# Folding conditioned weights by column half as they arrive, with the folded bias formed as columns

## The reference

```python
def _L0_cond_ref(x, y, weight, mask, bias):        # y: (2, 8), weight: (8, 256, 256)
    masked_w = weight * mask[None, :, :]
    w_bot = jnp.einsum('bg,got->bot', y, masked_w)
    return jnp.einsum('bnt,bot->bno', x, w_bot) + bias

x = x + _L0_attn_ref(_L0_cond_ref(x, cond_8, ...), wq, wk, wv, wo)   # 2 heads of 128, rotary on half of each, causal
x = x + _L0_ffn_ref(_L0_cond2_ref(x, cond_8, ...), Wg, W1, W2)
x = x + _L1_attn_ref(_L1_cond_ref(x, cond_8, ...), ...)
x = x + _L1_ffn_ref(_L1_cond2_ref(x, cond_8, ...), ...)
```

## Time and profile before

| | |
|---|---|
| median of 3 runs | 930.83 us (929.63 to 931.91) |
| the profiled execution | 928.71 us, span 927.4 us |
| TensorE busy | 911.9 us, 98% of the span |
| VectorE busy | 525.9 us, 57% |
| ScalarE busy | 443.8 us, 48% |
| GpSimd busy | 270.5 us, 29% |
| TensorE busy from 29 to 60 us | 29.37 of 31 us |
| VectorE busy from 5 to 25 us | 16.75 of 20 us |

### The profile page before, as it was taken

One profiled execution on the slowest core, in us unless ns is written; L12 is line 12 of the kernel. 1 busy time (PEld: TensorE's weight loads), 2 busy tenths in 40 slices (PEclk: granted clock), 3 DMA queues, 4 the chain that ended last, 5 costly groups with the idle time before them and its releaser, 6 DMA issues.

```text
span 927.4 us, 13114 instructions
## 1 busy us (share of the span) xinstructions
PE 911.9 (98%) x4859; PEld 768.5 (83%) x4859; DVE 525.9 (57%) x974; ACT 443.8 (48%) x827; POOL 270.5 (29%) x242
## 2 busy tenths in 40 slices
PE   8999999999999999999999999999999999999998
PEld 4768868887799999998888888888888888888886
DVE  6754454578657666686665564334333335787644
ACT  3665566434255455573444343353343443335775
POOL 1533221300466675654410162041140230010000
PEclk9999999999999999999999999999999999999999
DMA  8030001220355443432503003003003012000011
GB/s 301 30 114 23 24 2 69 103 85 24 81 127 177 137 134 127 126 114 81 181 23 139 21 23 136 1 1 136 1 0 137 1 38 99 1 0 1 1 46 46
DMA packets 22193, 67.47 MB, mean 73 GB/s; under 512 B 4515, under 2 KB 11955, under 8 KB 19315
## 3 DMA queue, kind: packets, MB, share of 16 engines
q1 hardware_dynamic: 16546, 40.15, 11.9%
q0 software_dynamic: 5440, 26.50, 9.7%
q10 hardware_dynamic: 144, 0.00, 0.0%
HBM read 55.09 MB, written 9.45 MB: 70 GB/s over the span
## 4 chain that ended last, share of the span: by engine, by line
PE 91%; DVE 4%; ACT 1%; DMA 1%; issue 1%; POOL 1%; SPq 0%; ACTq 0%; DVEq 0%; POOLq 0%
PE banks L1116 19%; PE banks L1118 19%; PE banks L1117 19%; PE banks L1378 5%; PE banks L1380 5%; PE banks L1379 5%; PE banks L1210 3%; PE banks L1194 2%; PE banks L1416 2%; PE banks L1417 2%; PE banks L1430 1%; PE banks L1429 1%; PE banks L1201 1%; PE banks L1285 1%; DMA weight_stage<-in_cond_w 1%
## 5 line engine op out<-in xcount | busy, mean ns | idle before, releaser
L1116 PE MATMUL banks<-input_hi,mlp_hi 128*128 128x512 f32 x376 | 147.6, 393 | 0.0
L1118 PE MATMUL banks<-input_hi,mlp_lo 128*128 128x512 f32 x376 | 146.5, 389 | 0.0
L1117 PE MATMUL banks<-input_lo,mlp_hi 128*128 128x512 f32 x376 | 146.4, 389 | 0.0
L1644 ACT CAST hidden_hi<-hidden 128x512 fp32r<-128x512 f32 x96 | 59.6, 621 | 159.1 <-DVE hidden L2065 107.0
L2254 POOL TENSOR_TENSOR mlp_lo<-weight_stage,mlp_hi 128x768 fp32r<-128x768 f32 x32 | 59.1, 1846 | 172.7 <-ACT mlp_hi L1622 172.7
L2071 DVE TENSOR_TENSOR hidden_lo<-hidden,hidden_hi 128x512 fp32r<-128x512 f32 x96 | 66.5, 692 | 61.7 <-ACT hidden_hi L1644 61.3
L2065 DVE SCALAR_TENSOR_TENSOR hidden<-banks,L_expert_weight,gelu 128x512 f32<-128x512 f32 x64 | 48.0, 750 | 83.6 <-PE banks L1118 80.4
L1638 ACT ACTIVATE gelu<-banks 128x512 f32<-128x512 f32 x96 | 57.4, 598 | 71.3 <-PE banks L1118 63.1
L1118 PEld LDWEIGHTS banks<-input_hi,mlp_lo 128*128 128x128 f32 x376 | 70.6, 188 | 14.8
L1116 PEld LDWEIGHTS banks<-input_hi,mlp_hi 128*128 128x128 f32 x376 | 70.6, 188 | 14.3
L1117 PEld LDWEIGHTS banks<-input_lo,mlp_hi 128*128 128x128 f32 x376 | 70.6, 188 | 14.3
(11 more groups left out here) (356 smaller groups left out, 2152.3 us busy)
## 6 DMA issues: line engine op xcount, KB each, us to landing
weight_stage<-in_packF SPq DMA_DIRECT2D x8, 1536.0 KB, 7.1
weight_stage<-in_shared SPq DMA_DIRECT2D x2, 3072.0 KB, 11.1
expert_output<-y_rows SPq DMA_DIRECT2D x40, 128.0 KB
weight_stage<-in_cond_w SPq DMA_DIRECT2D x4, 512.0 KB, 5.3
residual<-in_xT SPq DMA_DIRECT2D x4, 512.0 KB, 11.2
first_half_swapped<-first_half SPq DMA_DIRECT2D x16, 128.0 KB, 2.1
routed_input<-x_rows SPq DMA_DIRECT2D x16, 128.0 KB, 1.7
weight_stage<-in_ffn_w SPq DMA_DIRECT2D x2, 1024.0 KB, 8.7
```

Of the source, the lines that this page charges most:

```text
L1116: pe.matmul(o, wh, dh, start=(i == 0), stop=False)
L1117: pe.matmul(o, wh, dl, start=False, stop=False)
L1118: last = pe.matmul(o, wl, dh, start=False, stop=(i == len(terms) - 1))
L1644: act.copy(hiD[n % 4][:, :], prod_t[n % 2][:, :]).then_inc(done)
```

## The change

The summed weight, the mask and the staged groups are laid out by column half m (which is the row block m of the folded weight). `cw` becomes two units, `cw` 0 and `cw` 1, each eight groups and the mask over 256 columns instead of 512. `attn_qkv` is loaded first, then the groups of half 0 in three transfers (groups 0-2, 3-5, 6-7) with the mask ahead of the third, then those of half 1. `pick0` goes in front of the sums. TensorE folds row block 0 for both column halves a, then row block 1, all before the first projection. The bias is formed directly as six columns with the weights stationary, and the row form, its copy and its buffer go. There are 12 spins instead of 18, and HALF_ORDER becomes 6, 7, 4, 5, 0, 1, 2, 3.

```diff
+FIRST_GROUPS = (0, 3, 6)
-HALF_ORDER = [6, 7, 0, 1, 2, 3, 4, 5]
+HALF_ORDER = [6, 7, 4, 5, 0, 1, 2, 3]
-SPIN = {"weights of the fold": 18, "first rows": 24, "next rows": 4, }
+SPIN = {"weights of the fold": 12, "first rows": 24, "next rows": 4, }
...
+    def folded_rows(m):
+        for a in range(2):
+            product("out", "fold", 0, m, a)
+            act.append(("fold_hi", 0, m, a))
+            dve.append(("fold_lo", 0, m, a))
+            yield
...
-    dve.append(("cw",))
     act.append(("scale_q",))
     dve.append(("pick0",))
     use("out", [(n,) for n in range(8)])
     spin(SPIN["weights of the fold"], 4)
-    pe.append(("bias_row",))
-    banks["bias_row",] = (6, 7)
-    act.append(("row_in",))
+    product_of_bias()
+    for m in range(KD):
+        dve.append(("cw", m))
+    run(folded_rows(0))
     split_input(0)
-    run(folded(0, [0]))
+    run(folded_rows(1))
     run(conditioned_half(0, 4))
-    product_of_bias()
     split_input(1)
     first_swapped()
     for w in ("k", "q"):
         dve.append(("cosines", w, 0))
-    run(folded(0, [1]))
     first_rotated()
...
-            elif kind == "bias_row":
+            elif kind == "fold_bias":
                 pe.wait_ge(ld["cond"], 32)
                 pe.wait_ge(ld["aqkv"], 16)
-                for a in (1, 0):
-                    if a == 0:
+                for n in (2, 3, 4, 5, 0, 1):
+                    if n == 0:
                         pe.wait_ge(*ready("scale_q"))
                     for k in range(KD):
-                        last = pe.matmul(o[0:1, a * CH:a * CH + FH], bias_c[:, k:k + 1], aqkv[:, k, a * FH:(a + 1) * FH], start=(k == 0), stop=(k == KD - 1))
-                last.then_inc(done)
-            elif kind == "fold_bias":
-                pe.wait_ge(*ready("row_in"))
-                for n in range(FW // P):
-                    last = pe.matmul(o[:, n:n + 1], brow[:, n // 3, n % 3 * P:(n % 3 + 1) * P], ones32[0:1, 0:1], start=True, stop=True)
+                        last = pe.matmul(o[:, n:n + 1], aqkv[:, k, n * P:(n + 1) * P], bias_c[:, k:k + 1], start=(k == 0), stop=(k == KD - 1))
                 last.then_inc(done)
...
             elif kind == "cw":
-                w = cwF[0][:, :, :]
+                m, = key
+                w = cwF[0][:, m, :, :]
                 dve.wait_ge(ld["cond"], 32)
                 for g in range(G):
-                    if g % 2 == 0:
-                        dve.wait_ge(ld[f"cw{g // 2}"], 16)
+                    if g in FIRST_GROUPS:
+                        dve.wait_ge(ld[f"cw{3 * m + FIRST_GROUPS.index(g)}"], 16)
                     if g == 0:
-                        step(dve.tensor_scalar(w, cond_stage[:, 0, :, :], cond[:, 0, 0:1], None, ALU.mult))
+                        step(dve.tensor_scalar(w, cond_stage[:, m, 0, :, :], cond[:, 0, 0:1], None, ALU.mult))
                     else:
-                        step(dve.scalar_tensor_tensor(w, cond_stage[:, g, :, :], cond[:, 0, g:g + 1], w, ALU.mult, ALU.add))
+                        step(dve.scalar_tensor_tensor(w, cond_stage[:, m, g, :, :], cond[:, 0, g:g + 1], w, ALU.mult, ALU.add))
                 dve.wait_ge(ld["mask"], 16)
-                dve.tensor_tensor(w, w, cmask[:, :, :], ALU.mult).then_inc(done)
+                dve.tensor_tensor(w, w, cmask[:, m, :, :], ALU.mult).then_inc(done)
...
     def sync_program():
...
-        for i in range(4):
-            if i == 3:
-                sp.dma_start(aqkv[:, :, :], A["attn_qkv"]).then_inc(ld["aqkv"], 16)
-            sp.dma_start(cond_stage[:, 2 * i:2 * i + 2, :, :], A["cond_w"][:, 2 * i:2 * i + 2, :, :]).then_inc(ld[f"cw{i}"], 16)
-        sp.dma_start(cmask[:, :, :], A["cond_mask"]).then_inc(ld["mask"], 16)
+        sp.dma_start(aqkv[:, :, :], A["attn_qkv"]).then_inc(ld["aqkv"], 16)
+        for m in range(D // P):
+            for i, g in enumerate(FIRST_GROUPS):
+                gs = slice(g, (FIRST_GROUPS + (G,))[i + 1])
+                sp.dma_start(cond_stage[:, m, gs, :, :], A["cond_w"][:, m, gs, :, :]).then_inc(ld[f"cw{3 * m + i}"], 16)
+                if m == 0 and i == 1:
+                    sp.dma_start(cmask[:, :, :, :], A["cond_mask"]).then_inc(ld["mask"], 16)
```

More of the change, by code:

```diff
@@ L752 @@
 FREED = {
-    "bias_row": "row_in", "fold_bias": "bias_in", "fold": "fold_lo", "same": "same_in", "kept": "skip", "v": "v_row",
+    "fold_bias": "bias_in", "fold": "fold_lo", "same": "same_in", "kept": "skip", "v": "v_row",
     "S": "exp", "T": "p_col", "PV": "o_lo", "out": "resid",
@@ L765 @@
     "cosines": "rope_parts", "sines": "rope_parts",
-    "bias_row": "bias_product", "fold_bias": "bias_product", "row_in": "bias_in",
+    "fold_bias": "bias_product",
     "up": "into_hidden", "w1": "into_hidden", "gu": "into_hidden", "f1": "into_hidden",
@@ L907, in program @@
     sin_t = [sb("times_sin", [P, CH]) for _ in range(2)]
-    cwF = [sb("cond_weight", [P, KD, D]) for _ in range(B)]
-    cmask = sb("cond_mask", [P, KD, D])
-    brow = sb("bias_row", [1, 2, FH])
+    cwF = [sb("cond_weight", [P, D // P, KD, P]) for _ in range(B)]
+    cmask = sb("cond_mask", [P, D // P, KD, P])
     projected_top = top[0]
@@ L923, in program @@
     by_row = [sb("down_by_row", [P, ROW]) for _ in range(B)]
-    cond_stage = stage[:, 0:2048 * KD].rearrange("p (g k o) -> p g k o", k=KD, g=G)
+    cond_stage = stage[:, 0:2048 * KD].rearrange("p (m g k o) -> p m g k o", m=D // P, k=KD, g=G)
     top[0] = phase_top
@@ L1042, in program @@
         tail_at += n
-    names = ["cond", "cw0", "cw1", "cw2", "cw3", "small", "aqkv", "wo", "rope", "mask", "swap0", "swap1", "pack0_0", "pack0_1", "bdown", "mlp", "picked_mlp0", "picked_mlp1", "by_row", "gate_table", "gate_of_slot"]
+    names = ["cond", "cw0", "cw1", "cw2", "cw3", "cw4", "cw5", "small", "aqkv", "wo", "rope", "mask", "swap0", "swap1", "pack0_0", "pack0_1", "bdown", "mlp", "picked_mlp0", "picked_mlp1", "by_row", "gate_table", "gate_of_slot"]
     names += [f"x{c}" for c in range(NCH)] + [f"packF{i}" for i in range(2)] + [f"gather{i}" for i in range(ST + 1)]
@@ L1161, in tensor_program @@
                 pe.wait_ge(*ready("scale_q"))
-                pe.wait_ge(*(ready("half_mask") if b else ready("cw")))
+                pe.wait_ge(*(ready("half_mask") if b else ready("cw", m)))
                 for k in range(KD):
-                    last = pe.matmul(o[:, 0:FH], cwF[b][:, k, m * P:(m + 1) * P], aqkv[:, k, a * FH:(a + 1) * FH], start=(k == 0), stop=(k == KD - 1))
+                    last = pe.matmul(o[:, 0:FH], cwF[b][:, m, k, :], aqkv[:, k, a * FH:(a + 1) * FH], start=(k == 0), stop=(k == KD - 1))
                 last.then_inc(done)
@@ L1458, in scalar_program @@
                 act.activation(aqkv[:, :, FQ:FK], aqkv[:, :, FQ:FK], ACT.Copy, scale=1.0 / DH).then_inc(done)
-            elif kind == "row_in":
-                act.wait_ge(*ready("bias_row"))
-                act.copy(brow[:, :, :], bank(("bias_row",))[0:1, :].rearrange("p (a n) -> p a n", a=2)[:, :, 0:FH]).then_inc(done)
             elif kind == "bias_in":
@@ L1506, in scalar_program @@
                 elif n == 3:
-                    act.wait_ge(*ready("half", HALF_ORDER[1]))
-                    act.wait_ge(*ready("cw"))
+                    act.wait_ge(*ready("half", HALF_ORDER[3]))
+                    act.wait_ge(*ready("cw", 1))
                 act.wait_ge(*ready("max", c, h, i))
@@ L1748, in vector_program @@
             if kind == "pick0":
+                dve.wait_ge(ld["cond"], 32)
                 first_max(cond[:, :, :], B, m1, onehot, tm, s1)
@@ L2189, in pool_program @@
                 pool.wait_ge(*ready("pick0"))
-                pool.wait_ge(*ready("cw"))
+                pool.wait_ge(*ready("cw", 1))
                 pool.wait_ge(*ready("half_mask"))
@@ L2381 @@
         "cond_8": a["cond_8"],
-        "cond_w": a["L0_cond_weight"].reshape(G, KD, P, D).transpose(2, 0, 1, 3),
-        "cond_mask": cols(a["L0_cond_mask"], KD),
+        "cond_w": a["L0_cond_weight"].reshape(G, KD, P, D // P, P).transpose(2, 3, 0, 1, 4),
+        "cond_mask": a["L0_cond_mask"].reshape(KD, P, D // P, P).transpose(1, 2, 0, 3),
         "cond_bias": a["L0_cond_bias"].reshape(KD, P).T,
```

8 lines of the change are left out of this document (4 added, 4 removed).

## The result

The kernel after the change takes 934.5 us (median of 6 runs, 933.48 to 935.47), the kernel before 929.7 us (6 runs beside them, 927.68 to 931.91). The ratio is 1.0043, with a 95% interval of 1.0031 to 1.0055: the change makes the kernel slower by 0.4%. The forecast was 931.4 us, and its range went to 934.0. The profiled execution took 934.45 us for a span of 933.2, against the 928.71 and 927.4 of before, so 5.8 us of span are to be found. The median moved by 4.8 only. The profile of before is one of the kernel's runs with a mean granted clock of 1.000, and not all of its runs have that, as told under the experiments.

A forecast was written before the change was run, and what follows sets the result against it. Two chains, VectorE's and TensorE's, were taken to tie at the first score product, with VectorE nearly full. First piece +1.6, idle -1.4, split +2.2, `pick0` -1.9, fold wait +1.9, late folds -1.8 gave +0.6: 931.4 us, range 928.9 to 934.0.

The forecast's parts named there:

- Bytes: Loads at the start: first `cond_w` piece lands at 7.0 us, last at 11.9, and bytes no longer bind.
- the lag: Loads at the start: a piece lands when about 290 to 310 KB more than its own end have moved.
- t0: VectorE's conditioned weight sum: the time its half 1 is ready, forecast at 15.93 us.
- Split, `pick0`, folds: VectorE and TensorE start: split costs 2.2 us, hidden `pick0` saves 1.9, half 1's folds end at t0 + 2.97.
- the page's figures: VectorE's split sum: the Trainium skill's table gives 327 ns at 256 columns, so the split costs 0.5 us, not 2.2.
- The swap: Transfer of q's halves before its sines: lands in 2.1 us, ends at about 25.4, hidden by 0.3 only.
- The rope: VectorE's end before the first scores: sines and rope take 4.94 us, the same as before.
- S(0): First score product of attention chunk 0, starting at 29.42 us before the change and forecast at 30.04.
- TensorE's slack: TensorE ahead of S(0): its work ends at about 27.7 us, leaving over 2 us idle, a gain nobody collects.
- The clock rival: TensorE's bias and folds run at 1.2 GHz after spins end early: +0.9 to +6.5 us above the forecast; chance 0.12.
- Shift one for one: From S(0) to the kernel's end: the end moves by as much as S(0) does, forecast +0.6 us.

The follow-up runs named there:

- e2: The changed kernel with 18 spins instead of 12 ahead of the folds: 936.81 us, ratio 1.0049 to the kernel before.
- e3: The changed kernel with wo's low part moved behind attention chunk 0 on GpSimd: 933.83 us, ratio 1.0026 to the kernel before.
- a3: The changed kernel with the row bias, wo's low part behind the first attention and ten spins ahead of the first scores: 925.97 us, ratio 1.0015 on another chip.
- e1: The changed kernel with ten spins in front of the first score product: 933.62 us, ratio 1.0030 to the kernel before.
- e4: The kernel before with pick0 first, direct bias and all folds ahead of the first projection, but the sum 512 wide and not split: 937.28 us, ratio 1.0065.
- a1: The changed kernel with the old row form of the bias, its columns behind the folds of half 0: 933.87 us, ratio 1.0050 to the kernel before.
- a2: The changed kernel with six useless eight-column products ahead of the spins, to move TensorE's instruction fetch: 933.94 us, ratio 1.0065 to the kernel before.
- a4: The kernel of a3 with seven spins ahead of expert 0's second half of up products: 927.51 us, ratio 1.0035 to the kernel before.
- b1: The kernel before with only the direct bias, 24 one-column products behind 18 spins: 931.23 us, ratio 1.0020.
- b3: The kernel before with 40 useless eight-column products and 14 spins instead of 18, to move TensorE's instruction fetch: 926.15 us, ratio 1.0020 on its own chip.
- b2: The kernel before with 22 useless eight-column products and 15 spins instead of 18, to move TensorE's instruction fetch: 929.90 us, ratio 1.0006.
- b4: The kernel before with only seven spins ahead of expert 0's second half of up products: 926.32 us, ratio 1.0027.

## Where the prediction was right, where it was wrong, and why

The median lies 0.5 us above the range (928.9 to 934.0), though the range's upper end, a ratio of 1.0034, is inside the interval of the measured 1.0043. Slower was given 0.11. The forecast sum was +0.6; the span grew by 5.8.

**Bytes, half right.** The first piece came at 7.48, not at 7.0: by then 212 x 7.48 = 1586 KB had moved (0 to 7.48, mean 212 GB/s), so the lag was about 400 KB and not 292. The bytes bound nothing behind it. The passes were 0.11 us shorter than forecast, so t0 was 0.37 late (16.30 against 15.93), and that is what the path saw.

**Split, `pick0`, folds: right.** The two halves took 8.82 us (7.48 to 16.30), against 8.93 forecast from the 485 ns row. `pick0` was hidden. `half` began at 20.29, which is t0 + 3.99, exactly the formula (15.93 + 3.99 = 19.92, and t0 was 16.30). The fused operations' spacing of 0.52 also decides the matter of the page's figures: by those it would have been 0.36. (The 0.5 us that the prediction names for the split by these figures leaves out the nine further gaps of 0.035; with them it is 0.9.)

**The swap: this step failed.** The forecast said that it "ends at about 25.4 for q, just ahead of its sines at about 25.7, so it is hidden but by 0.3 only", with 2.1 us to land. It was issued at 24.23, 0.9 later than these figures mean, took 3.83, and the sines waited 2.08. Some 0.3 of that is the late issue: in e2, where this transfer took 2.1, the sines waited 0.28. The other 1.8 are the slow landing. The cover of 0.3 was named and no price was put on losing it. Of the 2.08, 0.98 came back: VectorE's rope of the keys now began just ahead of GpSimd's operation (28.87 against 28.99) and not behind one (25.80 against 25.32), and took 0.69 instead of 1.67.

**The rope: this step failed too.** "Sines and rope follow, 4.94 us" took the rope as before. But the rope now ran late enough for wo's low part to stand behind it in GpSimd's queue, and took 2.97 instead of 1.78, +1.2. e3 and a3, without wo's part there, have 1.76 and 1.75. With these terms S(0) closes: 0.62 + 0.37 + 2.08 - 0.98 + 1.19 = 3.28, and 3.29 was measured.

**TensorE's slack: this step failed the most instructively.** "With over 2 us of slack. That is a gain that nobody collects": it was 4.21 us, and it was not free. The clock fell 0.5 us behind its end, and the products behind S(0) paid 1.6 us. e1 (ten spins, a wait of 2.01 left) and e3 (the wait shortened to 2.91) both took the fall away and gave the 1.6 back: from S(0) to `down_by_row` it is 21.3 us in them and in the kernel before, 22.9 in the kernel after. All profiles agree: with 3.97 to 4.29 us of waiting (after, e2, e4, a1, a2) the clock fell between 0.8 us before S(0) and 0.6 behind it, and with 2.91 or less (e1, e3, a3, a4 and the kernels made from before, e4 aside) it didn't. The kernel before never waits more than some tenths there.

**The clock rival: right mechanism, wrong place.** It said that spins ending early and one-column products would let the clock fall over half 0's folds, and so it did (the window at 0.50). Which of the two does it isn't settled: in b1, with all 18 spins, the one-column products alone are followed by the fall, and in e2, with 18 spins and the same products, the clock stays at 1.00. It priced that at +0.9 to +3.7. It cost nothing, because half 1's folds wait for VectorE's second pass anyway: half 0's were over at 16.6, 0.3 behind t0. The same fall is worth 1.7 us in b1, where no pass covers it. The Trainium skill (TensorE: Matmul & The Clock Gate, Part 1) has the clock fall back after idleness; I wrote that the trace showed no fall, and let the chance lean on the spins alone. The falls around S(0) agree with the rule, and it would have pointed at the slack that my own sum had just found.

**Shift one for one: right** up to 250 us, apart from the clock. Behind that the third fall added 0.9 in the profile. It stands where expert 0 waits for its gather (1.72 us at 261.3 in the kernel after, 1.74 at 256.45 in the kernel before, there without a fall). Why it comes in the one and not in the other isn't settled: e2's profile, with the whole change and a wait of 1.73, has no third fall, and the kernel before has unprofiled runs with a fall somewhere. So the 0.9 can't be charged to the change.

**Why the swap was late.** In seven profiles with the instruction fetch inside the flight of q's last swap (after, e1, e3, e4, a1, a3, a4) that swap lands after 3.4 to 3.9 us. In three with the fetch between the issue of the first swap and the end of its packets (a2, e2, b3) the longest landing is 2.8, 2.7 and 2.4. In four with the fetch outside (before, b1, b2, b4) it is 2.1 to 2.5. a2 moved the one and the other followed. The packets say more. A swap is 80 packets. The DMA view of the kernel after, from 25.4 to 26.0 us (two lines), from 26.0 to 26.8 and from 26.8 to 28.0:

```profile
q1 hardware_dynamic: 75, 0.12, 55.7%
q8 instruction: 1, 0.02, 10.4%
...
DMA packets 0, 0.00 MB, mean 0 GB/s; under 512 B 0, under 2 KB 0, under 8 KB 0
...
q1 hardware_dynamic: 5, 0.01, 4.5%
```

75 packets are through by 25.97. The fetch's one packet lies from 25.82 to 26.82, and only then, from 26.80 to 27.61, come the last five, a sixteenth of the swap. It is the same in all seven: 75 packets in time, and five that begin within 0.02 us of the fetch's end (26.44 in e1, 26.69 in e3, 27.80 in e4, 25.87 in a1, 25.77 in a3, 26.20 in a4). So the share of one of the 16 DMA engines stood behind the fetch, by all that these records show; they don't name the engine. In the profiles with the fetch outside, all 80 move within 0.5 us.

**Still open.** What decides on the first and the third fall of the clock, and how much of the medians' 4.8 us the third one makes up.

## What to carry to other kernels

Slack that a change opens ahead of a dense stretch is not free: ask how long TensorE will stand idle there, and price the clock's fall, or fill the wait. When a chain moves by a few us, look up what stands behind its operations in the queue of the engine beside it: GpSimd's next operation can fall onto VectorE's last one. A cover of 0.3 us over a transfer whose landing time was read from a median is no cover; put the price of losing it into the sum as a case of its own.

## What the runs showed of the hardware that I had not expected

A 64x512 rope operation on VectorE takes 0.69 us when it starts ahead of GpSimd's, 1.66 to 1.78 when it starts behind one and waits for that one, and 2.97 when it waits for two. In the kernel after it ran from 29.48 to 32.45, and GpSimd's two from 28.99 to 31.90: VectorE finished 0.55 us behind them, as if it had done all of its work then. In the kernel before, GpSimd's two rope operations also stand in a row (25.32 to 28.62), but there VectorE's rope of the keys came in between them and ended at 27.47, 0.55 behind the first. Why it isn't let in between two in the kernel after, no run shows. The Trainium skill (Trainium Architecture — The Big Picture, "What this means for kernel authors") says that the pair's shared port is an exclusive lock and not a bandwidth split; these rows agree. In the seven slow swaps a single 16 KB packet of TensorE's instructions held up the last sixteenth of a transfer, which made it 1.4 to 1.9 us longer than the 2.0 of its neighbours.

Twenty-four one-column products in 2.95 us, busy as they look in the timeline, are followed by a clock of 0.50 over the folds behind them (b1, e1, e3, e4, a2, the kernel after), while the eight products of the row form, 384 columns wide, are not (a1, a3, a4, the kernel before and its other forms). But e2 has the same 24 products and its folds take 2.82 us at a clock of 1.00, so the products alone don't decide it.

The same kernel runs at medians of 924.5, 929.6 and 931.2 us on three chips, and at least one part of this has a place: expert 0's gathers were through 3.5 us sooner on the fastest.
